# Moving top-k exponentials and head sums between engines, with a new merge table, in a fused four-batch layer on one core

## What is computed

```
x = x + attention16(layernorm(x), ctx)        # 16 heads of width 8, softmax over 77 keys, output projection
x = x + experts(layernorm(x))                 # 8 experts 128 -> 512 -> 128, two chosen per token by a router
x = x + text_block(layernorm(x), ctx)         # below
x = x + int8_matmul(layernorm(x), rhs)        # row scales, round, clip, 128 x 128 product

# text_block: 4 heads, the 32 largest of 77 scores kept
scores = Q K^T / sqrt(32)                      # [512, 4, 77]
topv, topi = top_k(scores, 32)
attn_mean = mean over heads of scatter(softmax(topv))
c = attn_mean @ V ;  film factors = c @ W_film  (before and after the filter)
y = causal long convolution (by DFT) of the modulated layernorm(x)
h = x + modulated y ;  h = h + gelu(layernorm(h) @ W1 + b1) @ W2 + b2
return layernorm(h) * g_norm_out + b_norm_out
```

## Time and profile before

| | |
|---|---|
| median of three runs | 657.16 us |
| the profiled execution | 656.8 us |
| its span, first to last instruction | 655.0 us |
| mean granted TensorE clock | 0.863 |
| busy: PE, PEld, DVE, ACT, POOL | 527.0, 315.1, 452.9, 238.8, 132.9 us |

### The profile page before, as it was taken

The page is one execution under the profiler, slowest core; times in us unless marked ns, Lnnn a source line. Parts: engine busy times, 40 slices in busy tenths (PEclk is TensorE's granted clock), DMA queues, the critical chain, the costliest instruction groups (busy, mean ns, idle before and its releaser), DMA issues.

```text
span 655.0 us, 8058 instructions
## 1 busy us (share of the span) xinstructions
PE 527.0 (80%) x2539; PEld 315.1 (48%) x2539; DVE 452.9 (69%) x1770; ACT 238.8 (36%) x406; POOL 132.9 (20%) x164
## 2 busy tenths in 40 slices
PE   4539786297999999999999999999999973825360
PEld 2121133255545767445776435776767743323230
DVE  7379356548144447968668887979989879996516
ACT  3232551455433353444352446335273310501020
POOL 3502435333200120001032001215011151112210
PEclk9965555587999999999999999999999987776785
DMA  4519000012000020000012000000000000000000
GB/s 127 122 40 329 4 0 1 1 23 27 4 0 1 1 41 10 4 0 2 0 24 27 2 2 0 2 2 17 1 2 2 2 16 1 2 1 16 0 1 16
DMA packets 16156, 14.18 MB, mean 22 GB/s; under 512 B 1290, under 2 KB 14354, under 8 KB 16114
## 3 DMA queue, kind: packets, MB, share of 16 engines
q1 hardware_dynamic: 16114, 13.68, 8.4%
HBM read 8.86 MB, written 1.05 MB: 15 GB/s over the span
## 4 chain that ended last, share of the span: by engine, by line
PE 68%; DVE 16%; issue 5%; ACT 4%; SPq 3%; DMA 3%; POOL 1%; POOLq 0%; DVEq 0%; ACTq 0%
PE moe_y L765 17%; PE moe_h L753 16%; PE side L707 11%; PE side L697 3%; SPq L595 3%; PE side L805 3%; PE side L816 3%; DMA QA<-Q 3%; PE side L824 2%; PE side L832 2%; DVE area L1185 2%; PE side L793 1%; PE side L682 1%; PE side L630 1%; DVE TOP L1175 1%
## 5 line engine op out<-in xcount | busy, mean ns | idle before, releaser
L765 PEld LDWEIGHTS moe_y<-W,HT 128*128 128x128 f32 x1024 | 131.1, 193 | 45.7 <-issue 44.2
L765 PE MATMUL moe_y<-W,HT 128*128 128x128 f32 x1024 | 135.3, 277 | 0.0
L753 PE MATMUL moe_h<-xnT_moe,W 128*128 128x512 f32 x256 | 134.8, 615 | 0.0
L942 ACT ACTIVATE HT<-moe_h,W 128x512 f32<-128x512 f32 x128 | 87.4, 686 | 118.4 <-PE moe_h L753 118.3
L707 PE MATMUL side<-PT,VP 77*72 77x512 f32 x128 | 82.3, 733 | 4.6 <-ACT PT L924 4.6
L924 ACT ACTIVATE PT<-side 77x512 f32<-77x512 f32 x64 | 37.4, 591 | 53.8 <-PE side L697 53.5
L1161 DVE SCALAR_TENSOR_TENSOR X<-moe_y,RW,X 128x128 f32<-128x128 f32 x128 | 35.9, 343 | 20.7 <-PE moe_y L765 20.5
L753 PEld LDWEIGHTS moe_h<-xnT_moe,W 128*128 128x128 f32 x256 | 40.9, 196 | 12.5 <-issue 7.7
L1185 DVE MATCH_REPLACE8 area<-TOP,area 128x77 f32<-128x77 f32 x192 | 40.6, 224 | 0.0
L1446 POOL TENSOR_TENSOR area<-area 128x128 f32<-128x128 f32 x16 | 7.4, 460 | 162.8 <-ACT area L959 162.8
L697 PEld LDWEIGHTS side<-QA,KA 50*77 50x77 bf16 x64 | 7.0, 116 | 64.8 <-issue 59.1
(11 more groups left out here) (306 smaller groups left out, 838.0 us busy)
## 6 DMA issues: line engine op xcount, KB each, us to landing
W<-in_w SPq DMA_DIRECT2D x8, 512.0 KB, 7.5
QA<-Q SPq DMA_DIRECT2D x48, 64.0 KB
X<-in_x SPq DMA_DIRECT2D x4, 256.0 KB, 7.0
out_dram<-FO SPq DMA_DIRECT2D x4, 256.0 KB, 2.3
V<-in_vpack SPq DMA_DIRECT2D x1, 579.0 KB, 3.4
area<-in_r2pack SPq DMA_DIRECT2D x1, 576.0 KB, 6.4
area<-in_gpack SPq DMA_DIRECT2D x1, 576.0 KB, 4.5
FW<-in_dftf SPq DMA_DIRECT2D x1, 512.0 KB, 6.9
```

Of the source, the lines that this page charges most:

```text
L753: pe.matmul(moe_h[n % 2][:], W1[:, e, c * P:(c + 1) * P], xnT_moe[:, b % 2, :], start=True, stop=True).then_inc(moe_h_full, 1)
L765: mm = pe.matmul(moe_y[m % 2][:, t * P:(t + 1) * P], HT[:, m % 2, c, t * P:(t + 1) * P], W2[:, e, c, :], start=(c == 0), stop=(c == HC - 1))
L942: act.activation(HT[:, m % 2, c, :], moe_h[n % 2][:], ACT.Relu, bias=wc("b1")[:, e * HC + c:e * HC + c + 1]).then_inc(moe_h_ready, 1)
```

## The change

Five edits of the steps and a new merge table:

1. Top-k exponentials. VectorE's subtraction is gone. GpSimd negates the maxima of round 0 (128x4 values), and ScalarE computes four exponentials of 77 columns straight from PSUM, with the negated maximum of the head as bias. It waits for the negation, for the four replaces of round 0, and for the buffer's last use two tiles back; and it, no longer VectorE, releases the bank.
2. The sum over heads. One multiplication over 4x77 columns by the spread factors and one reduction that reads the four heads with a stride of 77 elements replace the four instructions.
3. Head sums. ScalarE copies the 8x512 sums; TensorE spreads them; VectorE takes the reciprocal of the spread 128x512 block in PSUM and multiplies. Two reciprocals of 8x512 per batch become one of 128x512.
4. Output norm. Gain and bias are merged: (x - mean) * gain, then times the inverse deviation plus X, four instructions each. GpSimd has added the bias to X before, in the `dft` step.
5. The last residual addition moves to GpSimd for batches 0 to 2.

```diff
 ORDER = """
...
-E3 O T5 E2 T2 E4 T4 E3 O2 T E T E2 O T O E6 T O T E7 T E O E11 T3 O3 T3 O T3 O3 T O T O T4 O T11 O T2 O T O T2 O T2
-O2 T O18
+T3 O T O E4 O T E2 T3 E2 O E10 T2 E T2 E3 T3 E O E2 O E8 T E T O E O3 E12 T O2 T O T3 O2 T2 O T11 O T4 O T O T3 O T3
+O T2 O T O18
...
                 if kind == "attn_sum":
                     src, read = filled(act, "pv", b, 0, i)
-                    act.wait_ge(rz_ready, 2 * b + i + 1)
+                    if b >= 1:
+                        emptied(act, "attn_norm", b - 1, 0)
+                    act.activation(ZR[i][64:GROWS, :], src[64:GROWS, :], ACT.Copy).then_inc(rz_ready, 1)
                     act.activation(OV[64 * i:64 * i + 64, :], src[0:64, :], ACT.Copy).then_inc(read, 1)
...
                 if kind == "topk" and i[1] == 0:
                     n = b * T + i[0]
-                    act.wait_ge(top_diff, n + 1)
-                    act.activation(TE[:, n % 2], TE[:, n % 2], ACT.Exp).then_inc(top_exp, 1)
+                    a = n % 2
+                    src, read = filled(act, kind, b, i[0])
+                    act.wait_ge(top_neg, n + 1)
+                    if n >= 2:
+                        act.wait_ge(top_acc, n - 1)
+                    act.wait_ge(top_rep, (n * TOPR + 1) * H1)
+                    for h in range(H1):
+                        ins = act.activation(TE[:, a, h, :], src[:, h * NK:(h + 1) * NK], ACT.Exp, bias=NM[:, a, h:h + 1])
+                    ins.then_inc(read, 1)
...
                     if i == "out":
-                        dve.wait_ge(ln_out["out"], b + 1)
-                        y = xnorm["out"][:]
-                        dve.tensor_tensor(y, y, rc("go").unsqueeze(1).broadcast_to((P, T, D)), ALU.mult).then_inc(out_a, 1)
-                        dve.wait_ge(out_a, 2 * b + 1)
-                        dve.tensor_tensor(y, y, rc("bout").unsqueeze(1).broadcast_to((P, T, D)), ALU.add).then_inc(out_a, 1)
-                        dve.wait_ge(out_a, 2 * b + 2)
-                        dve.tensor_tensor(y, y, X[:, b], ALU.add).then_inc(x5_ready, 1)
+                        if b >= 1:
+                            dve.wait_ge(out_ready, b)
+                        y = xnorm["out"]
+                        for t in range(T):
+                            ins = dve.scalar_tensor_tensor(y[:, t, :], src[:, t, :], mv[i][:, t, 0:1], rc("go"),
+                                                           ALU.subtract, ALU.mult)
+                        ins.then_inc(ln_out[i], 1)
+                        dve.wait_ge(ln_out[i], b + 1)
+                        dve.wait_ge(xo_ready, b + 1)
+                        for t in range(T):
+                            ins = dve.scalar_tensor_tensor(y[:, t, :], y[:, t, :], rstd[i][:, t:t + 1], X[:, b, t, :],
+                                                           ALU.mult, ALU.add)
+                        ins.then_inc(x5_ready, 1)
...
-                if kind == "attn_sum":
-                    src, _ = filled(dve, "pv", b, 0, i)
-                    if b >= 1:
-                        emptied(dve, "attn_norm", b - 1, 0)
-                    dve.reciprocal(ZR[i][64:GROWS, :], src[64:GROWS, :]).then_inc(rz_ready, 1)
                 if kind == "attn_norm":
...
-                    dve.tensor_tensor(OT[:], src[:], OV[:], ALU.mult).then_inc(read, 1)
+                    dve.reciprocal(OT[:], src[:]).then_inc(zi_ready, 1)
+                    dve.wait_ge(zi_ready, b + 1)
+                    dve.tensor_tensor(OT[:], OT[:], OV[:], ALU.mult).then_inc(read, 1)
...
-                    if r == 0:
-                        dve.wait_ge(top_max, (n * TOPR + 1) * H1)
-                        dve.tensor_tensor(TE[:, a], src[:, 0:H1 * NK].rearrange("p (h k) -> p h k", h=H1),
-                                          TOP[:, a, :, 0, 0:1].broadcast_to((P, H1, NK)), ALU.subtract)\
-                           .then_inc(top_diff, 1)
...
-                    for h in range(H1):
-                        if h == 0:
-                            dve.tensor_scalar(AM[:, a, 0:NK], TE[:, a, h, :], TZ[:, a, 2, h:h + 1], None, ALU.mult)\
-                               .then_inc(top_acc, 1)
-                        else:
-                            dve.wait_ge(top_acc, n * H1 + h)
-                            dve.scalar_tensor_tensor(AM[:, a, 0:NK], TE[:, a, h, :], TZ[:, a, 2, h:h + 1], AM[:, a, 0:NK],
-                                                     ALU.mult, ALU.add).then_inc(top_acc, 1)
+                    dve.tensor_tensor(TE[:, a], TE[:, a], TZ[:, a, 2, :].unsqueeze(2).broadcast_to((P, H1, NK)), ALU.mult)\
+                       .then_inc(top_mul, 1)
+                    dve.wait_ge(top_mul, n + 1)
+                    dve.tensor_reduce(AM[:, a, 0:NK], TE[:, a].rearrange("p h k -> p k h"), AX, ALU.add).then_inc(top_acc, 1)
...
+                if kind == "topk" and i[1] == 0:
+                    n = b * T + i[0]
+                    a = n % 2
+                    pool.wait_ge(top_max, (n * TOPR + 1) * H1)
+                    if n >= 2:
+                        emptied(pool, "topk", (n - 2) // T, (n - 2) % T)
+                    pool.tensor_scalar(NM[:, a, :], TOP[:, a, :, 0, 0], -1.0, None, ALU.mult).then_inc(top_neg, 1)
...
+                if kind == "dft":
+                    pool.wait_ge(ln_out["text"], 2 * (b + 1))
+                    pool.tensor_tensor(X[:, b], X[:, b], rc("bout").unsqueeze(1).broadcast_to((P, T, D)), ALU.add)\
+                        .then_inc(xo_ready, 1)
...
+                if kind == "quant_mm" and b < B - 1:
+                    emptied(pool, kind, b, i)
+                    pool.tensor_tensor(FO[:], FO[:], xnorm["out"][:], ALU.add).then_inc(out_ready, 1)
```

72 lines of the change are left out of this document (36 added, 36 removed).

## The result

The changed kernel took 665.42 us (median of four runs, 664.61 to 666.65), the kernel before 657.19 on the same chip: a ratio of 1.012, 95% interval 1.0098 to 1.0142. It is 8.2 us slower; the forecast was 9 us faster. The profiled execution took 666.04 us with a span of 664.0, against 655.0 before.

A forecast was written before the change was run, and what follows sets the result against it. TensorE was taken to bound 200 to 526.1 us, VectorE the tail to 597.2. Terms 5.3 - 6.4 - 5.7 - 1.0 + 0.1 - 1.5 = -9.2 us gave 647.6, for the median 648.0; range 641.5 to 657.

The forecast's parts named there:

- Start of the argument: TensorE bounds 200 to 526.1 us, VectorE 526.1 to 597.2; freeing VectorE gains nothing directly before 526.1.
- Moved TensorE work: Five TensorE steps move from behind the last expert to in front of it, which then ends 5.3 us later.
- Waits for Q's DMAs: TensorE's 4.9 us of waits in batches 1 and 3 shrink as more expert steps fill them: net -1.5 us.
- Exponentials on ScalarE: Four biased activations per tile, 1.1 us instead of 0.46, cost nothing because the result is needed over 4 us later.
- Rival (b): ScalarE's queue delays experts' activations; 1.5 us in each of 12 tiles before 526, 666 us; chance 0.10.
- signs of being wrong: TensorE waits for ScalarE's HT between 200 and 526, or a tail longer than 65 us.
- Start of the tail: From last expert to first maximum of batch 3: 11.3 us instead of 17.7, -6.4.
- Rest of the tail: First maximum of batch 3 to its DFT: -7.7 us against a new wait of 2.0, net -5.7.
- rival (d): The strided reduction over heads takes twice 0.48 us: 4 x 0.5 in the tail, 650 us; chance 0.07.
- Last batch: The chain behind 597.2 us keeps all but its output norm: -1.0 us.
- Prologue: Batch 0's bare head-sum chain: multiplication over at 103.9 us instead of 103.8, +0.1 (-1 to +1.5).
- Head sums: One 128-row reciprocal replaces two of 8 rows; VectorE's saving in batches 1 to 3 falls under TensorE's work.

The follow-up runs named there:

- e8: Changed kernel, six expert steps moved in front of smax of batches 2 and 3, and film.1.0 moved later: 656.1 us, ratio 0.9970.
- e9: Changed kernel, ScalarE issues a tile's top-k exponentials behind the AMT copy of the tile before (11 of 16 tiles): 662.3 us, ratio 1.0067.
- e1: Kernel before with all five edits but its old merge table: 666.3 us, ratio 1.0152.
- e14: Changed kernel, six expert steps moved in front of smax of batches 2 and 3, film.1.0 untouched: 665.8 us, ratio 1.0115.

## Why the prediction was wrong, point by point

**Start of the argument.** That TensorE bounds the dense stretch and VectorE the tail held. So did the conclusion that a freed VectorE gives nothing in the dense stretch.

**Moved TensorE work, +5.3.** Right in the main: in e8 the lines of the moved work (L811, L799, L845, L853) are busy for 5.9 us more than before, of 6.2 in all.

**Waits for Q's DMAs, -1.5: the first step that failed.** They rose from 4.9 to 7.9 us. I counted the expert steps between Q's DMAs and `smax` in batches 1 and 3, found more of them than before, and booked a gain. In batch 1 it came (3.69 to 2.94). In batch 3 the DFT of batch 0 (3.5 us) had also stood in front of `smax` and does no longer: from Q's product (L679) on TensorE has 13.4 us of work to cover the way instead of 14.1, and the wait is 2.57 instead of 1.24. Batch 2 I did not count at all, and there the count would not have been enough. TensorE has nearly the same work in front (14.6 us, 14.9 before, when nothing waited), but Q lands later:

```profile
243.28 7.90 SPq L601 DMA_DIRECT2D QA<-Q  x12
256.98 0.96 PE L688 MATMUL side<-KM,QA 128*128 128x154 bf16 x8 [2.35 <-DMA QA<-Q]
```

The first DMA is issued 3.2 us behind the start of Q's product instead of 2.6, with an expert's activation now between ScalarE's Q instructions, and `smax` starts 13.7 us after that issue instead of 12.3. Why the DMAs themselves took longer is open. So two sums count: the TensorE time in front of the waiting instruction, and the way to the landing of the data with what stands in it.

**Exponentials on ScalarE, 0: the second.** I asked only what waits for the exponentials and whether experts' activations stand behind them. The `AMT` copy stands behind them too, and the new table put a FiLM product right there: 3.94 us. Rival (b) named the queue and its 666 lies beside the measured 665.4, but by luck: it is made of 1.5 us in each of 12 tiles, where one tile of the dense stretch lost 3.94. Neither of the forecast's signs of being wrong showed: TensorE had no wait for `HT`, and the tail is shorter than 65 us.

**The clock, not in the sum at all: the third.** The earlier trace rows showed 1.00 from 200 us on, and I took full-clock durations without asking what new gaps would do. The same work took up to 5 us longer in the dense stretch. e8 returned 9.3 us for 6.6 of idle time removed. Four stretches of the changed kernel (columns as in the first view):

```profile
257.00:262.00 5.00, 5.00 (x33) 3.77 (x34) 3.38 (x7) 0.60 (x1) 0.00 (x0) 0.66 0.01 3
364.00:369.00 5.00, 4.59 (x36) 3.63 (x37) 3.55 (x9) 0.69 (x1) 0.00 (x0) 1.00 0.00 0
389.00:394.00 5.00, 4.70 (x22) 4.25 (x23) 0.46 (x5) 0.86 (x4) 0.91 (x2) 0.66 0.00 0
437.00:442.00 5.00, 5.00 (x20) 3.30 (x20) 3.81 (x2) 0.86 (x2) 0.00 (x0) 0.66 0.00 0
```

The first follows the Q wait of 2.35, the third the FiLM gap of 3.94, and both are at 0.66. The second follows the Q wait of 2.57 and is at 1.00. The last is at 0.66 and no wait of TensorE is shown in front of it since the FiLM gap, 48 us earlier. So a gap does not always bring the clock down, and it can fall without one.

**Start of the tail, -6.4.** Measured -4.4. The inverse DFT and the text norm came as forecast (norm over at 551.3, 6.7 after the last expert); the way from there to the scores took 6.5 instead of 4.5, since transposition, projection and scores ran at the low clock (L778 2.04 us, 1.10 before).

**Rest of the tail, -5.7.** Measured -5.2. The reduction over heads takes 0.675 us, not 0.48 (rival (d) true in kind, 0.2 a tile instead of 0.5). FiLM products wait 3.93 and 4.48 us in this stretch too, but these waits are hardly on its path: in e9 they are 0.41 and 0.45, and its tail is 61.0 instead of 61.4.

The Trainium skill, SBUF — State Buffer, says in its section on the DMA port swizzle that each access crossing to a new line pays. The trace does not speak against it: 675 ns with elements 77 apart (L1220), 474 for 308 elements in a row (L1204). But L1220 also writes 77 sums a row and L1204 four, and no run parts the two.

**Last batch, -1.0.** The norm gave it: e1, e8 and e14 end in 56.5 to 56.8. In the changed kernel the end ran at a clock of 0.68 instead of 0.71 and took 58.1.

**Prologue, +0.1.** Measured +1.2. The reciprocal over 128 rows takes 3.36, as taken; the 1.2 is the multiplication beside GpSimd.

**Head sums, nothing in batches 1 to 3.** Right for the new table: the waits of its dense stretch have none for the multiplication. It has five expert steps in between in batch 1, and four with tile work among them in batches 2 and 3. What I missed is that this was the edit for which the table was needed: it costs 7 to 9 us with the old one, and the new one 35 without it.

## What to carry to other kernels

When a table of steps moves work, recount for every wait the time of everything that now stands in front of the waiting instruction, and on each in-order engine what stands ahead of the small copy that feeds the next product. Allow for more than the length of a gap on a full TensorE: here removing 6.6 us of idle time gave 9.3, though removing 3 of them alone (e14) gave nothing. Measure a change of code and a change of order crossed, each with and without the other: here the two interact by about 40 us, and either comparison alone would have misled.
